# A hand-written order of TensorE's work in an attention kernel: V's product, the small turns, and stretches of three score tiles

## The reference, cut to what matters

```python
# x: (16, 512, 256).  16 heads of 16; K and V are shared by all heads.
xn = layernorm(x)
q  = (xn @ Wq.T + bq) * 16 ** -0.5            # (16, 512, 256) -> (16, 16*512, 16)
k, v = split(xn @ Wkv.T + bkv)                # (16, 512, 16) each
attn = softmax(q.reshape(16, 8192, 16) @ k.T) @ v
attn = heads_to_channels(attn) @ Wo.T + bo
# expert part: one of 6 experts is picked per token by its largest gate logit
gate   = one_hot(argmax(xn @ w_gate))
tokens = einsum('elr,erc->elc', A, B)         # 6 experts, 100 tokens, 256 channels
p      = softmax(xn . tokens * 256 ** -0.5)   # over the 100 tokens
delta  = ((p[1:] @ (tokens @ wt.T + wt_b)[1:] + xn) @ wd.T + wd_b) * scale
out    = x + attn + xn + log(sum_e exp(delta) * gate)
```

## Time and profile before

| | |
|---|---|
| median of 3 runs | 893.94 us (892.45 to 893.95) |
| the profiled execution | 893.1 us, its span 891.3 us |
| TensorE busy | 837.5 us, 94% of the span |
| VectorE busy | 770.9 us, 86% |
| ScalarE busy | 687.0 us, 77% |
| GpSimd busy | 566.8 us, 64% |
| mean granted TensorE clock | 0.973 of full speed (2.4 GHz), and 1.00 from 80 to 850 us |
| one batch in the steady part | 51.44 us |

### The profile page before, as it was taken

One profiled execution on the slowest core, in us unless ns is written; L12 is line 12 of the kernel. 1 busy time (PEld: TensorE's weight loads), 2 busy tenths in 40 slices (PEclk: granted clock), 3 DMA queues, 4 the chain that ended last, 5 costly groups with the idle time before them and its releaser, 6 DMA issues.

```text
span 891.3 us, 18198 instructions
## 1 busy us (share of the span) xinstructions
PE 837.5 (94%) x6038; PEld 276.6 (31%) x6038; DVE 770.9 (86%) x1488; ACT 687.0 (77%) x1386; POOL 566.8 (64%) x754
## 2 busy tenths in 40 slices
PE   6679999999999999999999999999999999999987
PEld 4333223332323332332323233232333333232213
DVE  7688898989989898998989899898989899898926
ACT  2226888888888888888888878888887888888883
POOL 2874677676667767666677766667775766646321
PEclk7688999999999999999999999999999999999989
DMA  4413243634433443534444453443435345241112
GB/s 118 116 41 66 68 101 86 131 86 127 102 97 86 121 107 97 126 93 107 91 109 107 104 120 86 120 98 91 113 97 120 86 119 112 62 105 62 63 52 71
DMA packets 125076, 86.09 MB, mean 97 GB/s; under 512 B 57143, under 2 KB 109112, under 8 KB 124984
## 3 DMA queue, kind: packets, MB, share of 16 engines
q1 hardware_dynamic: 124504, 84.56, 38.5%
q10 hardware_dynamic: 480, 0.36, 0.1%
HBM read 39.30 MB, written 33.54 MB: 82 GB/s over the span
## 4 chain that ended last, share of the span: by engine, by line
PE 76%; DVE 14%; issue 4%; POOL 3%; ACT 2%; DMA 1%; DVEq 0%; POOLq 0%
PE pO L376 24%; PE pA L358 18%; PE pB L363 8%; DVE M L850 8%; PE pA L499 5%; PE pA L446 5%; PE pA L518 4%; PE pA L501 3%; PE pA L435 3%; PE pA L471 2%; PE pA L486 2%; ACT P L658 2%; DVE st L778 1%; PE pB L479 1%; DVE RL L863 1%
## 5 line engine op out<-in xcount | busy, mean ns | idle before, releaser
L850 DVE TENSOR_REDUCE M<-pA 128x1 f32<-128x512 f32 x1024 | 650.0, 681 | 80.3 <-PE pA L358 79.0
L658 ACT ACTIVATE P<-pB 128x512 f32<-128x512 f32 x1002 | 556.5, 605 | 124.8 <-PE pB L363 120.5
L358 PE MATMUL pA<-K,Q 48*128 48x512 f16 x1024 | 320.3, 388 | 27.0 <-DVE M L850 15.0
L363 PE MATMUL pB<-Q,K 50*128 50x512 f16 x1002 | 314.0, 385 | 0.3 <-DVE M L850 0.2
L376 PE MATMUL pO<-P,VK 128*32 128x512 f32 x2048 | 273.9, 607 | 2.0 <-ACT OTr L664 1.1
L358 PEld LDWEIGHTS pA<-K,Q 48*128 48x128 f16 x1024 | 67.8, 94 | 337.7 <-DVE M L850 273.7
L1005 POOL TENSOR_TENSOR Rs<-Rs,Cz 128x512 f32<-128x512 f32 x32 | 40.7, 1272 | 51.1 <-ACT Cz L646 49.0
L376 PEld LDWEIGHTS pO<-P,VK 128*32 128x32 f32 x2048 | 40.6, 108 | 96.7 <-issue 56.8
L998 POOL TENSOR_SCALAR Cz<-Cx 128x512 f32<-128x512 f32 x32 | 62.1, 1941 | 11.5 <-ACT Cx L640 11.5
L363 PEld LDWEIGHTS pB<-Q,K 50*128 50x128 f16 x1002 | 64.1, 94 | 7.4 <-ACT P L658 5.5
L963 POOL CAST Qp<-qf 128x512 f16<-128x512 f32 x31 | 18.9, 610 | 66.4 <-ACT qf L607 66.3
(11 more groups left out here) (170 smaller groups left out, 897.5 us busy)
## 6 DMA issues: line engine op xcount, KB each, us to landing
o_parts<-OTr SPq DMA_DIRECT2D x62, 256.0 KB, 2.2
X<-in_x SPq DMA_DIRECT2D x16, 512.0 KB, 3.9
q_pieces<-Qp SPq DMA_DIRECT2D x64, 128.0 KB
out<-OUT SPq DMA_DIRECT2D x32, 256.0 KB, 3.4
Op<-o_parts SPq DMA_DIRECT2D x31, 256.0 KB
Rb<-l_parts SPq DMA_DIRECT2D x31, 256.0 KB
Q<-q_pieces SPq DMA_DIRECT2D x30, 256.0 KB, 4.7
Q<-q_pieces SPq DMA_DIRECT2D x34, 128.0 KB, 4.6
```

The source lines that it names most:

```text
L358: e.matmul(bank1("ab", t)[:, :], Q16[r:r + 48, b % 3, h, 128 * s:128 * s + 128], K16[r:r + 48, b % 3, :], start=True, stop=True).then_inc( ...
L363: e.matmul(bankB(t)[:, :], K16[r:r + 50, b % 3, 128 * i:128 * i + 128], Q16[r:r + 50, b % 3, :, 32 * hh:32 * hh + 32], start=True, stop=Tr ...
L658: e.activation(P[:, u % PR, :], bankB(u + LB)[:, :], ACT.Exp, scale=alpha).then_inc(S("e"))
L850: e.tensor_reduce(M[:, t // 32 % 2, t % 2, t % 32 // 2:t % 32 // 2 + 1], bank1("ab", t)[:, :], AX, ALU.max, negate=True).then_inc(S("mx"))
```

## The change

It alters the order on TensorE in these places, where k is the slot within a batch's 64:

- `vg` moves from slot 19 to right behind the P times V of slot 17, and from the ring `pB` to the ring `pA`.
- `vt` moves from slot 27 to right behind `q1`, which moves from 23 to 20.5; `p` from 51 to right behind `o3`; `mt` in the middle of the batch from right behind `o2` to right ahead of it. `mt` becomes 128 by 128: its input `M2` is made 128 columns wide, of which 64 are zero.
- Score tiles stood in pairs. Three times a batch, six of them now stand as two stretches of three (18 to 23, 34 to 39, 50 to 55), with the displaced small product between the two, and the P times V that stood between pairs (21, 37, 53) behind the second (23.5, 39.5, 55.5).
- `d2` moves from 39 to 27 (not in the first batch, where `a`, `d0`, `d1` move instead).
- The evictions follow. On VectorE `gate` is cut into its five steps, `gate0` at 27.8 to `gate4` at 31.3, with maxima between them.

```diff
-    "kd": -41.6, "vg": -45, "vge": -44.3, "q1": -41, "qe1": -39.4, "qs1": -38.2, "qw1": -35.6,
-    "vt": -37, "vte": -36.4, "gate": -34.8, "mask": -32.6, "mkd": -31.4,
+    "kd": -41.6, "vg": -46.9, "vge": -46.3, "q1": -43.5, "qe1": -42.3, "qs1": -38.2, "qw1": -35.6,
+    "vt": -43.4, "vte": -41.3, "gate0": -36.2, "gate1": -35.2, "gate2": -34.2, "gate3": -33.2, "gate4": -32.7,
+    "mask": -32.2, "mkd": -31.4,
...
+STRETCH = (0, 2, 4, 6, 8, 10, 12, 14, 16, 18, 21, 24, 26, 28, 30, 32, 34, 37, 40, 42, 44, 46, 48, 50, 53, 56, 58, 60, 62)
+PV_AT = {5: 3.5, 9: 3.5, 13: 3.5}
...
+    def stretch(n):
+        k = n % 64
+        first = max(m for m in STRETCH if m <= k) if n < NT else k - k % 4
+        return n - k + first + 0.02 * (k - first)
+
     for n in range(NT + LB):
-        put("ab", n - n % 2 + 0.02 * (n % 2) if n < NT else n - n % 4 + 0.02 * (n % 4), n)
+        put("ab", stretch(n), n)
...
     for v in range(NT // 4):
-        put("pv", 4 * (v + LV + (v + LV >= NT // 4)) + 1, v)
+        k = v + LV + (v + LV >= NT // 4)
+        put("pv", 4 * k + (PV_AT.get(k % 16, 1) if k < NT // 4 else 1), v)
...
-        M2 = sb("M2", [128, 2, 2, H], F16)
+        M2 = sb("M2", [128, 128], F16)
...
-            "a": lambda b: (S("mm"), b + 1), "rg": lambda b: (S("two"), 2), "bs": lambda b: (S("scl"), 1),
+            "a": lambda b: (S("mm"), b + 1), "vg": lambda b: (S("vge"), b + 1), "rg": lambda b: (S("two"), 2), "bs": lambda b: (S("scl"), 1),
...
-                    e.transpose(bank2("mt", g)[:, :].bitcast(F16)[0:64, 0:128],
-                                M2[:, :, :, :].rearrange("p a k h -> p (a k h)"), idh[:, :]).then_inc(S("mt"))
+                    w.wait_ge(S("mz"), 1)
+                    e.transpose(bank2("mt", g)[:, :].bitcast(F16)[:, 0:128], M2[:, :], idh[:, :]).then_inc(S("mt"))
```

More of the change, by code:

```diff
@@ L41 @@
     "residual": 10.2, "q0": -53, "qe0": -51.4, "qs0": -46.5, "qw0": -44, "uk": -49, "uke": -47.4, "ks": -44.2,
-    "kd": -41.6, "vg": -45, "vge": -44.3, "q1": -41, "qe1": -39.4, "qs1": -38.2, "qw1": -35.6,
-    "vt": -37, "vte": -36.4, "gate": -34.8, "mask": -32.6, "mkd": -31.4,
[2 rows of a table added]
+    "mask": -32.2, "mkd": -31.4,
     "qread": -25.8, "utm": -24.9, "s": -21,
-    "smax": -20.4, "sexp": -18.8, "ssum": -17.4, "snorm": -16.2, "p": -13, "pte": -12.4, "a": -5, "mm": -4.4,
+    "smax": -20.4, "sexp": -18.8, "ssum": -17.4, "snorm": -16.2, "p": -11.4, "pte": -10.8, "a": -5, "mm": -4.4,
     "d0": -1, "dexp0": -0.4, "d1": 3, "dexp1": 3.6, "guard0": 6.1, "dlog0": 12.2, "radd0": 15.9,
[3 rows of a table removed]
[3 rows of a table added]
 }
@@ L52 @@
     "q0": -57, "qe0": -56, "qs0": -55, "qw0": -54, "uk": -53, "uke": -52, "ks": -51, "kd": -50, "q1": -52, "qe1": -51,
-    "qs1": -50, "vg": -50, "vge": -50.5, "vt": -48, "vte": -47, "gate": -46, "mask": -45, "qw1": -40, "mkd": -39,
-    "utm": -30, "s": 9, "smax": 9.6, "sexp": 10.2, "ssum": 10.8, "snorm": 11.4, "p": 17, "pte": 17.6, "a": 21, "mm": 21.6,
-    "d0": 25, "dexp0": 25.6, "d1": 29, "dexp1": 29.6, "guard0": 30.8, "dlog0": 34.2, "radd0": 35.6,
+    "qs1": -50, "vg": -50, "vge": -50.5, "vt": -48, "vte": -47, "gate0": -46, "gate1": -45.9, "gate2": -45.8, "gate3": -45.7, "gate4": -45.6, "mask": -45, "qw1": -40, "mkd": -39,
+    "utm": -30, "s": 9, "smax": 9.6, "sexp": 10.2, "ssum": 10.8, "snorm": 11.4, "p": 17, "pte": 17.6, "a": 23.6, "mm": 24.2,
+    "d0": 29, "dexp0": 29.6, "d1": 31, "dexp1": 31.6, "guard0": 32.8, "dlog0": 36.2, "radd0": 37.6,
+    "d2": 39, "dexp2": 39.6,
 }
@@ L89 @@
 DVE_NAMES = ("rngq", "rng", "two", "scl", "wl", "scd", "stats0", "stats1", "stats2", "stats3", "aggr", "refine", "xl0", "xl1",
-             "qs0", "gate", "smax", "ssum", "mm", "mx", "rec", "fo0", "fo1", "fo2",
+             "qs0", "gate0", "gate1", "gate2", "gate3", "gate4", "smax", "ssum", "mm", "mx", "rec", "fo0", "fo1", "fo2",
              "fo3", "nl00", "nl01", "nl02", "nl03", "nl10", "nl11", "nl12", "nl13")
@@ L265, in build @@
         ld = nc.dram_tensor("l_parts", (4, 8 * T), F32, kind="Internal").ap()
+        M2v = M2[:, 0:64].rearrange("p (a k h) -> p a k h", a=2, k=2)
         def bc(ap, n):
@@ L291, in build @@
         FREED2 = {
-            "ab": lambda t: (S("e"), t - LB + 1), "vg": lambda b: (S("vge"), b + 1),
+            "ab": lambda t: (S("e"), t - LB + 1),
             "vt": lambda b: (S("gt"), b + 1), "p": lambda b: (S("pte"), b + 1),
@@ L450, in _ @@
                 if (b := due("vg", n)) is not None:
-                    w.wait_ge(*before2("vg", b))
+                    w.wait_ge(*before1("vg", b))
                     w.wait_ge(*turned(b))
@@ L456, in _ @@
                             for i in range(4):
-                                mm = e.matmul(bank2("vg", b)[32 * i:32 * i + 32, 0:128], wcP[:, wp, c, V0:V0 + 32],
+                                mm = e.matmul(bank1("vg", b)[32 * i:32 * i + 32, 0:128], wcP[:, wp, c, V0:V0 + 32],
                                               xT[:, b % 2, i, xp, c, :], start=(k == 0 and c == 0), stop=(k == 2 and c == 1))
@@ L807, in _ @@
                     e.tensor_tensor(Qp[:, 0, 1, :], qf[:, 0, :], Qp[:, 0, 0, :], ALU.subtract).then_inc(S("ql0"))
-                if (b := due("gate", n)) is not None:
+                if (b := due("gate0", n)) is not None:
                     w.wait_ge(S("gt"), b + 1)
                     e.tensor_reduce(gmx[:, :], G[:, :, :], AX, ALU.max).then_inc(S("g0"))
+                if (b := due("gate1", n)) is not None:
                     w.wait_ge(S("g0"), b + 1)
                     e.tensor_tensor(geq[:, :, :], G[:, :, :], bc(gmx[:, :], NE), ALU.is_equal).then_inc(S("g1"))
+                if (b := due("gate2", n)) is not None:
                     w.wait_ge(S("g1"), b + 1)
@@ L817, in _ @@
                                     ALU.mult).then_inc(S("g2"))
+                if (b := due("gate3", n)) is not None:
                     w.wait_ge(S("g2"), b + 1)
                     e.tensor_reduce(gm2[:, :], gw[:, :, :], AX, ALU.max).then_inc(S("g3"))
+                if (b := due("gate4", n)) is not None:
                     w.wait_ge(S("g3"), b + 1)
@@ L882, in _ @@
             e.memset(mk[:, :, ER:128], 1.0).then_inc(S("mk1"))
+            e.memset(M2[:, 64:128], 0.0).then_inc(S("mz"))
             w.wait_ge(S("id"), 2)
```

6 lines of the change are left out of this document (3 added, 3 removed), and 6 rows, old and new, of the table SLOT.

## The result

| | before | after |
|---|---|---|
| median | 894.29 us, 8 runs (892.45 to 894.99) | 902.53 us, 7 runs (896.22 to 906.87) |
| the profiled execution's span | 891.3 us | 900.7 us |
| its mean granted TensorE clock | 0.973 | 0.964 |
| ratio after to before | | 1.0078 [1.0054, 1.0102] |

A forecast was written before the change was run, and what follows sets the result against it. TensorE was taken to bound the kernel, at 51.44 us a batch. Adding 3.55 and removing 3.10 gives +0.45 a batch, +6.3 over 14 windows, +0.3 for start and end: 900.5 us from 893.94, range 890.5 to 906.5.

The forecast's parts named there:

- the 6.3 us that it had for the batches: +0.45 us a batch over the 14 of 16 windows where tiles A and B run and a next batch is prepared.
- keys' products 51.9 apart: Sign in the changed kernel's timeline: the keys' products of successive batches start 51.9 us apart, before 51.44.
- The bound: TensorE, busy 94% of the span, read by distances between starts: 51.44 us a batch, 2.41 of it waits.
- four old waits: TensorE's waits around V's product (0.59), V's turn (0.78), at `o1` (0.68), around `p` (0.36): all go, 2.41 us a batch.
- The stretches: Six score tiles as two threes cost 1.54 us instead of 1.62 as pairs, three times a batch: 0.24 gained.
- The shapes: Five boundaries between TensorE products of different shape go, 0.09 us each: 0.45 a batch; bounds nothing and 0.12 each.
- Tile 23: It waits for ScalarE's copy of the gate logits, queued behind exponentials of tiles 21 and 22: 2.08 us a batch.
- The later waits: New TensorE waits at P times V of slot 33, `mt` at 35.2, tiles 38 and 39, tile 55: 0.32, 0.43, 0.32, 0.40 us.
- the later waits do not come: Rival: waits at slot 33, tiles 38 and 39, and tile 55 vanish; batch gains 0.59 us, 885.9 us; chance 0.13.
- shape changes cost more than 0.09: Rival: at 0.12 us per shape change a batch loses 0.30, giving 898.4 us, about no change; chance 0.15.
- 3.55 - 3.10 = +0.45 us a batch: Sum for a steady batch: 3.55 us of new waits less 3.10 of waits, stretches and shapes that go.
- together +0.3, give or take 1: First window (later `a`, `d0`, `d1` delay GpSimd's work ahead of the first `mt`) and last window, in us.

## Why the prediction was right in the number and wrong in its parts

Predicted were 900.5 us and slower; measured 902.53 and slower by 0.8%. But that is luck: the 6.3 us that it had for the batches are not there, and what is there instead, the clock above all, it had not named. Its own sign, keys' products 51.9 apart, did not come; they are 51.43 apart. Point by point, from the undisturbed batch of the changed kernel (starts at 310.14 and 361.57).

**The bound** was read rightly: distances between starts on TensorE explain the batch before and after. All four old waits went: V's product costs 0.45 (312.96 to 313.41), its turn 0.20 (315.53 to 315.73) where 0.26 was taken, and `o1` and `p` have no wait ahead of them. 2.41 stands.

**The stretches** gave what they should: three tiles cost 0.76 where nothing waits, and 0.77 was forecast. That makes 0.27 a batch against 0.24.

**The shapes**, forecast 0.45 with a bound of 0.12 each. Measured 0.53: P times V to `vg` 0.12 (0.88 against 1.00), `q1` to `vt` 0.09, `o3` to `p` 0.10 (340.10 to 340.76 against 0.76), `mt` with `o2` 0.12, `d1` to `mt` 0.10. The last is the difference of these rows. Timeline of TensorE, before:

```profile
345.53 0.60 PE L501 MATMUL pA<-W,MmT 98*128 98x256 f32 x2
346.06 0.24 PE L507 MATMUL pB<-idh,M 128*64 128x128 f16 x1
```

after:

```profile
352.57 0.60 PE L514 MATMUL pA<-W,MmT 98*128 98x256 f32 x2
353.00 0.22 PE L521 MATMUL pB<-idh,M 128*128 128x128 f16 x1
```

A boundary is worth 0.09 to 0.12, near the upper bound. The constant of 166 ns, from which the prediction had estimated 0.83 by the Trainium skill ("TensorE: Matmul & The Clock Gate", Single matmul latency), is too high here: each of the five gave less, and in the kernel with `mt` 128 wide alone a boundary gave 0.10 (`o2`) and 0.12 (`d1` with `mt`). Turns behind a product of their own shape are also shorter themselves, `vt` by 0.05 and `p` by 0.04 (0.54 against 0.57), which the sum did not have.

**Tile 23**, forecast 2.08, start 2.54 behind tile 21: measured 2.54, and 2.10 of wait. The count along ScalarE's queue was exact.

**The later waits**, forecast 0.32, 0.43, 0.32 and 0.40, all came, three of them smaller. Timeline of TensorE after, from the pair ahead of the P times V of slot 33 to that of 39.5:

```profile
325.70 0.39 PE L371 MATMUL pA<-K,Q 48*128 48x512 f16 x1
...
326.48 1.07 PE L389 MATMUL pO<-P,VK 128*32 128x512 f32 x8 [0.18 <-ACT P L671]
327.48 0.39 PE L371 MATMUL pA<-K,Q 48*128 48x512 f16 x1
...
328.59 0.23 PE L521 MATMUL pB<-idh,M 128*128 128x128 f16 x1 [0.28 <-ACT P L671]
...
329.41 0.39 PE L371 MATMUL pA<-K,Q 48*128 48x512 f16 x1
...
330.34 1.06 PE L389 MATMUL pO<-P,VK 128*32 128x512 f32 x8
```

The plain cost is 0.54 for a pair and 0.76 for three tiles. By the unrounded starts, 0.78 is 0.25 of wait, 1.11 is 0.35, 0.93 is 0.18, and at tile 55 1.15 is 0.40. The three tiles behind `vg` wait 0.06 for `vge`, forecast as nothing. Together that is 1.24 where 1.47 was forecast. So the rival "the later waits do not come" is refuted: of its 1.04 at the slots 33, 38, 39 and 55, 0.83 came. The rival "shape changes cost more than 0.09" is right in direction and gave 0.08 of the 0.46 by which a batch is shorter than forecast.

**The step that failed** is the prediction's line "3.55 - 3.10 = +0.45 us a batch". Measured it is 3.34 that comes and 3.31 that goes (2.41 + 0.27 + 0.53 + 0.10 for the shorter turns), and the batch is 0.01 shorter. The mechanism of each term was right and its size was not: the later waits were 0.23 too large, the shapes 0.08 too small, the shorter turns (0.10) were taken as nothing, and the stretches were 0.03 too small. All of these err to the same side, and only tile 23's wait, 0.02 larger than forecast, to the other. The 0.04 between these sums and the distance of the keys' products is in no term of this list; rounding can make it.

**The second step that failed** is "together +0.3, give or take 1", for the start and the end. The first window lost 2.63 and the second 0.54. The prediction had seen that `a`, `d0` and `d1` delay what stands ahead of the first `mt`, and gave it next to nothing. The first `mt` is 2.8 later (65.73 against 62.92). With it the granted clock of the window fell from 0.87 to 0.82, and for the clock the prediction had no term.

**What was missing** is the clock. The prediction treated a wait of 2.1 us as 2.1 us. Half of the loss, 4.65 us in the profiled run, comes from three batches in which TensorE ran at 1.2 GHz for a while behind that wait. Only one execution has a trace. By the mean clocks of the others the falls vary from run to run, and this is the likely reason why one execution of this kernel takes 896 us and another 907. Without the three falls the profiled run would stand at 897.9, beside the fastest runs of 896.2 and 897.2. The number was right because errors offset each other. Forecast were 6.3 for the batches and 0.3 for start and end, and measured are 0 for the batches, 2.63 + 0.54 for the first two windows, 4.65 for the clock and 0.67 + 0.90 for start and end.

## What to carry to other kernels

Before tiles are moved on the engine that sets the time, follow the readers' queue: who must empty the bank, and what stands ahead of it there. Here one number, the slot of a small copy on ScalarE, was the difference between 0.8% slower and 2.3% faster, and none of the parts that a run took back or tried alone had made the steady part slower. The moves of V's product, of its turn and of `o2` were not tried alone. A wait on TensorE costs just its length only as long as the granted clock stays up; where runs of a kernel scatter more than those of its neighbour, look at the clock by windows before looking for a spread in the work. Moves that are right for the steady part want a price of their own in the first window, where other engines set the time.

## What the runs showed of the hardware that was not expected

- A single idle of 1.93 us in a batch was followed by a fall of the granted clock to 1.2 GHz in 3 of 14 batches, one of 0.78 us in none. With one of 2.4 us the clock fell in 7 of 14, in three of them within the idle itself. A fall cost 1.5 us, and 2.8 in the three that began within the idle.
- A change between products of different shapes cost 0.09 to 0.12 us on TensorE at the five places measured, and the turn with 64 output rows beside products with 128 paid it too. 64 zero columns more in `M2` made the product ahead of `mt` cheaper by 0.10.
